# A post-layernorm layer on one core: setup loads as rows, clip logarithms in pieces, and waits by operand

## The reference

```
r = sigmoid(x Wr^T);  k = x Wk^T;  v = x Wv^T
dec = sigmoid(decay);  scale[t] = exp(t * log(clip(dec, 1e-7)))
cum = cumsum(k * v / clip(scale, 1e-10));  state = cum * scale
y = rmsnorm(r * state) * ln_w;  x1 = layernorm(x + y Wo^T)
h = gelu(x1 bw1^T + b1);  out = layernorm(x1 + h bw2^T + b2)
```

## Time and profile before

| | |
|---|---|
| median of 3 runs | 822.54 us (822.36 to 822.7) |
| the profiled execution | 822.86 us |
| its span | 821.0 us |
| busy in the span: PE, DVE, ACT, POOL | 798.2, 772.6, 678.9, 295.6 us |
| granted clock of PE, mean | 0.998 |

### The profile page before, as it was taken

How to read it: one execution, slowest core, us unless ns; L and a number is a source line. 1 busy time by engine, 2 the same in 40 slices (tenths; PEclk the granted TensorE clock), 3 DMA queues, 4 the chain that set the end, 5 groups by cost and what they waited for, 6 DMA issues and landing times.

```text
span 821.0 us, 16564 instructions
## 1 busy us (share of the span) xinstructions
PE 798.2 (97%) x5173; PEld 505.3 (62%) x5173; DVE 772.6 (94%) x1467; ACT 678.9 (83%) x971; POOL 295.6 (36%) x570
## 2 busy tenths in 40 slices
PE   6989999999999999999999999999999999999986
PEld 4555666656666656666656666665666665666653
DVE  7998999999999999999999999999999999999886
ACT  7887888888888888888888888888888888887775
POOL 3343323344323344233344333344332334332344
PEclk9999999999999999999999999999999999999999
DMA  8413554444553434554434554444455344444313
GB/s 249 91 46 78 129 113 94 102 103 102 128 128 83 110 88 102 128 128 92 113 80 109 118 128 103 102 90 108 109 128 112 93 98 106 102 102 103 78 33 97
DMA packets 169847, 86.27 MB, mean 105 GB/s; under 512 B 130145, under 2 KB 165473, under 8 KB 169825
## 3 DMA queue, kind: packets, MB, share of 16 engines
q1 hardware_dynamic: 148304, 52.97, 29.8%
q0 software_dynamic: 4608, 16.78, 10.8%
q10 hardware_dynamic: 16912, 16.26, 5.8%
HBM read 20.45 MB, written 16.78 MB: 45 GB/s over the span
## 4 chain that ended last, share of the span: by engine, by line
PE 89%; DVE 4%; POOL 2%; issue 2%; ACT 2%; DMA 1%; POOLq 0%; DVEq 0%; ACTq 0%; SPq 0%
PE ps_r L362 28%; PE ps_o L483 26%; PE ps_f L433 19%; PE ps_r L433 6%; PE ps_o L388 6%; PE ps_o L393 3%; DVE hid_lo L981 1%; DMA x_in<-in_L_attn_x_dram 1%; DVE u L932 1%; ACT hid L662 1%; DVE u_st L940 0%; PE ps_s L370 0%; POOL root L1284 0%; POOL y_sqs L1272 0%; ACT hid_hi L697 0%
## 5 line engine op out<-in xcount | busy, mean ns | idle before, releaser
L483 PE MATMUL ps_o<-w2T,hid_hi 128*128 128x256 f16 x992 | 218.9, 273 | 3.4 <-DVE hid_lo L981 3.0
L483 PE MATMUL ps_o<-w2T,hid_lo 128*128 128x256 f16 x992 | 218.8, 273 | 0.0
L362 PE MATMUL ps_r<-x_t,proj_hi 128*128 128x512 f16 x768 | 197.1, 379 | 1.7 <-DVE proj_lo L1057 1.2
L433 PE MATMUL ps_f<-x_t,w1T 128*128 128x512 f16 x768 | 181.7, 379 | 1.6 <-DVE x_t L965 1.3
L662 ACT ACTIVATE hid<-ps_f,b1c,f_scale 128x512 f32<-128x512 f32 x192 | 145.3, 774 | 41.6 <-PE ps_f L433 36.6
L981 DVE SCALAR_TENSOR_TENSOR hid_lo<-hid,hid_scale,hid_hi 128x1024 f16<-128x1024 f32 (+1 forms) x136 | 160.3, 1222 | 0.9 <-POOL hid_hi L1305 0.6
L1272 POOL TENSOR_TENSOR y_sqs<-y_sq 128x512 f32<-128x512 f32 x32 | 46.7, 1459 | 308.4 <-ACT y_sq L637 308.4
L362 PEld LDWEIGHTS ps_r<-x_t,proj_hi 128*128 128x128 f16 x768 | 74.5, 98 | 92.1 <-issue 3.4
L697 ACT ACTIVATE hid_hi<-hid,hid_scale 128x2048 f16<-128x2048 f32 (+2 forms) x72 | 128.0, 1778 | 3.2
L433 PEld LDWEIGHTS ps_f<-x_t,w1T 128*128 128x128 f16 x768 | 74.9, 98 | 79.6 <-issue 1.6
L362 PE MATMUL ps_r<-x_t,proj_lo 128*128 128x512 f16 x384 | 114.2, 379 | 0.0
(11 more groups left out here) (182 smaller groups left out, 1333.0 us busy)
## 6 DMA issues: line engine op xcount, KB each, us to landing
x_in<-in_L_attn_x_dram SPq DMA_DIRECT2D x32, 512.0 KB, 4.4
res<-b_row POOLq DMA_DIRECT2D x32, 512.0 KB, 4.6
out_dram<-res ACTq DMA_DIRECT2D x31, 512.0 KB, 3.1
w_in<-in_L_ffn_w_dram SPq DMA_DIRECT2D x2, 1024.0 KB, 10.2
x_t<-x_st SPq DMA_TRANSPOSE x59, 4.3
b_row<-in_L_ffn_b_dram SPq DMA_DIRECT2D x1, 512.0 KB, 13.2
proj_in<-in_L_attn_Wk_dram SPq DMA_DIRECT2D x1, 256.0 KB, 5.2
proj_in<-in_L_attn_Wv_dram SPq DMA_DIRECT2D x1, 256.0 KB, 5.4
```

What stands on the lines that cost most here:

```text
L362: last = nc.tensor.matmul(ps_r[:, m, :], w[:, m, dc, ec * P:(ec + 1) * P], xx[:, :, dc, :], start=(n == 0), stop=(n == 3 * DC - 1))
L433: last = nc.tensor.matmul(f1_bank[hc % NF], w1T[:, hc, dc, :], xx[:, :, dc, :], start=(dc == 0 and n == 0), stop=(dc == DC - 1 and n == 1))
L483: last = nc.tensor.matmul(o_tok[:, tt, :], hh[:, hc, tt * P:(tt + 1) * P], w2T[:, :, hc, :], start=(hc == 0 and n == 0), stop=(hc == HC - ...
```

## The change

decay, ln_w and b1 are loaded by ACT as 2 + 2 + 8 rows of 128 elements into one tile `rows`; PE turns it with one transpose to 128 x 12 (its first instruction, which waits for all three), and DVE copies that from PSUM to `rows_c`, of which decay, ln_w and b1 are now columns. SP issues the load of x first, and its semaphore instructions after the load of x of chunk 2; b1 is no longer in its queue. The squares of chunk 0 move from ACT to DVE. The transposes of chunk 0 go 6 and 2 around the sum of the bound, before 4 and 4, and into banks 1 and 2 of ps_r. clip_g's logarithms are made in four pairs of 512 columns (`clip_logs(n)`), three in the setup and one in the prologue before k_sb of chunk 1; clip_table(0) stands behind proj_split_hi(0). R of chunk 0 waits for proj_hi first, for x lo and for proj_lo only before the products that read them.

```diff
             load(0, 0, 0)
...
             load(2, 0, 2)
-            sp.dma_start(b1c[:, :], b1.rearrange("(c p) -> p c", p=P),
-                         allow_slow_non_contiguous=True).then_inc(s_b1_in, 16)
+            for n in range(CPB):
+                sp.sem_inc(s_stored[n], 16)
+            sp.sem_inc(s_zout, TT)
+            sp.sem_inc(s_xt, 16)
+            sp.sem_inc(s_x1t, 16)
+            sp.sem_inc(s_zadd, 1)
...
                         if first and not ec:
-                            pe.wait_ge(s_setup_ev, m + 1)
+                            pe.wait_ge(s_proj_hi, m + 1)
+                            if m:
+                                pe.wait_ge(s_xl, c + 1)
                         n = 0
                         for w, xx in ((proj_hi, x_split[slot][0]), (proj_hi, x_split[slot][1]),
                                       (proj_lo, x_split[slot][0])):
+                            if first and not ec and not m and n == DC:
+                                pe.wait_ge(s_xl, c + 1)
+                            if first and not ec and n == 2 * DC:
+                                pe.wait_ge(s_setup_ev, m + 1)
...
             def prologue():
+                n = 2 * DC + HC
                 pe.wait_ge(s_ident, 1)
+                pe.wait_ge(s_rows_in, 48)
+                nc.tensor.transpose(ps_rows, rows[:, :], ident[0:n, 0:n]).then_inc(s_rows_t, 1)
                 pe.wait_ge(s_x_in[0], 16)
-                transposes(x_bank[0][:, 0:DC, :], x_in[0], 0, (0, 1))
+                transposes(x_bank[0][:, 0:DC, :], x_in[0], 0, (0, 1, 2))
                 sum_xbound(0)
-                transposes(x_bank[0][:, 0:DC, :], x_in[0], 0, (2, 3)).then_inc(s_tx, 1)
+                transposes(x_bank[0][:, 0:DC, :], x_in[0], 0, (3,)).then_inc(s_tx, 1)
...
-            act.dma_start(dec_c[:, 0, :], decay.rearrange("(c p) -> p c", p=P),
-                          allow_slow_non_contiguous=True).then_inc(s_decay_in, 16)
-            act.dma_start(lnw_c[:, :], ln_w.rearrange("(c p) -> p c", p=P),
-                          allow_slow_non_contiguous=True).then_inc(s_lnw_in, 16)
-            act.wait_ge(s_decay_in, 16)
-            nc.scalar.activation(dec_c[:, 1, :], dec_c[:, 0, :], ACT.Sigmoid).then_inc(s_setup_a, 1)
+            for row, w in ((0, decay), (DC, ln_w), (2 * DC, b1)):
+                n = HC if row == 2 * DC else DC
+                act.dma_start(rows[row:row + n, :], w.rearrange("(c p) -> c p", p=P)).then_inc(s_rows_in, 16)
+            act.wait_ge(s_rows, 1)
+            nc.scalar.activation(dec_c[:, 0, :], rows_c[:, 0:DC], ACT.Sigmoid).then_inc(s_setup_a, 1)
...
             nc.scalar.activation(warm[:, :], ones_col[:, :], ACT.Exp)
-            xsq(0, 0, 0, first=True)
...
             def clip_table(n):
 
-                act.wait_ge(s_clip, DC)
+                act.wait_ge(s_clip, DC * n + DC)
...
             def prologue():
-                clip_table(0)
                 xh(0, 0)
                 proj_split_hi(0)
+                clip_table(0)
                 proj_split_hi(1)
                 clip_table(1)
                 proj_split_hi(2)
...
+            def clip_logs(n):
+
+                dve.wait_ge(s_const, 1)
+                dve.wait_ge(s_setup_a, 2)
+                part = slice(n * CH, (n + 1) * CH)
+                for dc in range(DC):
+                    nc.vector.tensor_scalar(clip_g[:, dc, part], steps[:, part], dec_c[:, 1, dc:dc + 1], -LOG_CLIP,
+                                            ALU.mult, ALU.min).then_inc(s_clip, 1)
+
+            dve.wait_ge(s_rows_t, 1)
+            nc.vector.tensor_copy(rows_c[:, :], ps_rows).then_inc(s_rows, 1)
             dve.wait_ge(s_setup_a, 1)
-            nc.vector.tensor_scalar_max(dec_c[:, 1, :], dec_c[:, 1, :], CLIP_DEC).then_inc(s_setup_v, 1)
...
+            nc.vector.tensor_scalar_max(dec_c[:, 0, :], dec_c[:, 0, :], CLIP_DEC).then_inc(s_setup_v, 1)
+            dve.wait_ge(s_x_in[0], 16)
+            nc.vector.scalar_tensor_tensor(out=x_sq[:, :, :], in0=x_in[0][:, :, :], scalar=1.0, in1=x_in[0][:, :, :],
+                                           op0=ALU.mult, op1=ALU.mult,
+                                           accum_out=bounds[:, DC:DC + 1]).then_inc(s_xsq, 1)
+            proj_maximum(0)
             take_xbound(0, 0)
-            proj_maximum(0)
+            clip_logs(0)
             proj_scale(0)
             proj_maximum(1)
             xl(0, 0)
             proj_scale(1)
             proj_split_lo(0)
             proj_maximum(2)
+            clip_logs(1)
             proj_split_lo(1)
             proj_scale(2)
...
+            clip_logs(2)
             proj_split_lo(2)
...
                 take_bounds(0, 2)
+                clip_logs(3)
                 dve.wait_ge(s_exp, 2 * DC)
                 kvs(1, 1, 0)
```

More of the change, by code:

```diff
@@ L96, in postln_layer_kernel @@
         steps = sb("steps", [P, T])
-        lnw_c = sb("lnw_c", [P, DC])
-        dec_c = sb("dec_c", [P, 3, DC])
+        rows = sb("rows", [2 * DC + HC, P])
+        rows_c = sb("rows_c", [P, 2 * DC + HC])
+        lnw_c = rows_c[:, DC:2 * DC]
+        b1c = rows_c[:, 2 * DC:2 * DC + HC]
+        dec_c = sb("dec_c", [P, 2, DC])
         log_clip = sb("log_clip", [P, 1])
@@ L170, in postln_layer_kernel @@
         o_last = ps_r[:, 0:2, :].rearrange("p a (b d) -> p (a b) d", d=D)
-        x_bank, x_split = [ps_r, ps_o, ps_f], [(x_hi, x_lo), (x1_hi, x1_lo), (x_hi, x_lo)]
+        x_bank, x_split = [ps_r[:, 1:3, :], ps_o, ps_f], [(x_hi, x_lo), (x1_hi, x1_lo), (x_hi, x_lo)]
         ps_sums = ps_s[:, 0:TT * TT]
@@ L177, in postln_layer_kernel @@
         ps_wmax = ps_s[:, TT * TT + DC + 1:TT * TT + DC + 7]
+        ps_rows = ps_s[:, P // 2:P // 2 + 2 * DC + HC]
         ps_womax = ps_f[:, 0, 0:2]
@@ L185, in postln_layer_kernel @@
         s_wo_in, s_w1_in, s_w2_in = (sem(n) for n in ("wo_in_s", "w1_in_s", "w2_in_s"))
-        s_decay_in, s_lnw_in, s_b1_in, s_b2_in = (sem(n) for n in ("decay_in_s", "lnw_in_s", "b1_in_s", "b2_in_s"))
+        s_rows_in, s_rows_t, s_rows, s_b2_in = (sem(n) for n in ("rows_in_s", "rows_t_s", "rows_s", "b2_in_s"))
         s_zeroed, s_ident, s_const = sem("zeroed_s"), sem("ident_s"), sem("const_s")
@@ L264, in load @@
                 sp.dma_start(x_in[j][:, :, :], x_v[c]).then_inc(s_x_in[j], 16)
-            for n in range(CPB):
-                sp.sem_inc(s_stored[n], 16)
-            sp.sem_inc(s_zout, TT)
-            sp.sem_inc(s_xt, 16)
-            sp.sem_inc(s_x1t, 16)
-            sp.sem_inc(s_zadd, 1)
             load(0, 0, 0)
@@ L344, in R @@
                 pe.wait_ge(s_xh, c + 1)
-                pe.wait_ge(s_xl, c + 1)
+                if not first:
+                    pe.wait_ge(s_xl, c + 1)
                 for ec in ecs:
@@ L664, in gelu, with xsq @@
                                          scale=f1_scale[:, hc:hc + 1]).then_inc(s_gelu, 1)
-            def xsq(c, b, j, first=False, looped=False):
+            def xsq(c, b, j, looped=False):
                 act.wait_ge(s_x_in[j], 16 * b + 16)
@@ L670, in xsq @@
                     act.wait_ge(s_bounds, c - 2)
-                elif not first:
+                else:
                     act.wait_ge(s_xbounds, c)
@@ L1069, in _ @@
                                     ALU.add).then_inc(s_fold, 1)
-            dve.wait_ge(s_decay_in, 16)
-            dve.wait_ge(s_setup_a, 1)
-            nc.vector.tensor_scalar_max(dec_c[:, 1, :], dec_c[:, 1, :], CLIP_DEC).then_inc(s_setup_v, 1)
-            dve.wait_ge(s_const, 1)
-            dve.wait_ge(s_setup_a, 2)
-            for dc in range(DC):
-                nc.vector.tensor_scalar(clip_g[:, dc, :], steps[:, :], dec_c[:, 2, dc:dc + 1], -LOG_CLIP, ALU.mult,
-                                        ALU.min).then_inc(s_clip, 1)
+            def clip_logs(n):
[7 more added lines that the diff above has]
+            nc.vector.tensor_copy(rows_c[:, :], ps_rows).then_inc(s_rows, 1)
+            dve.wait_ge(s_setup_a, 1)
+            nc.vector.tensor_scalar_max(dec_c[:, 0, :], dec_c[:, 0, :], CLIP_DEC).then_inc(s_setup_v, 1)
[4 more added lines that the diff above has]
+            proj_maximum(0)
             take_xbound(0, 0)
-            proj_maximum(0)
+            clip_logs(0)
             proj_scale(0)
@@ L1093, in wo_maxima @@
                 dve.wait_ge(s_wo_in, 16)
-                dve.wait_ge(s_lnw_in, 16)
+                dve.wait_ge(s_rows, 1)
                 nc.vector.tensor_reduce(w_max[:, 3:4], wo_in[:, :, :], AX.XY, ALU.max,
@@ L1357, in _ @@
             for dc in range(DC):
-                nc.gpsimd.tensor_scalar(decay_f[:, dc, :], steps[:, 0:CH], 0.0, dec_c[:, 1, dc:dc + 1],
+                nc.gpsimd.tensor_scalar(decay_f[:, dc, :], steps[:, 0:CH], 0.0, dec_c[:, 0, dc:dc + 1],
                                         ALU.mult, ALU.add)
```

6 lines of the change are left out of this document (3 added, 3 removed).

## The result

The changed kernel takes 823.51 us (median of 20 runs, 823.38 to 824.38), the kernel before 822.46 (20 runs in turn with them, 822.31 to 822.70). The ratio is 1.0015, 95% interval 1.0008 to 1.0022: 1.05 us or 0.13% slower, inside the 0.2% that the prediction called no change, and 0.2 us from its 823.3. The profiled execution took 823.39 us with a span of 821.6.

The account below looks back on a forecast made before the run. DVE's setup work up to k_sb of chunk 1 was taken to set the end: 5.71 + 17.25 + 1.28 + 0.38 + 3.6 + 0.3 = 28.52 against 27.62, 0.9 later, so 823.3 us; range 820.8 to 825.3.

Parts of the forecast that it names:

- the long row: PE's long row of second FFN products after the setup, starting at 63.93 before the change, forecast near 64.8.
- What bounds: Setup: DVE runs nearly unbroken from k_sb of chunk 1 to PE's long row, so a k_sb shift moves the end.
- Start of the squares, 5.71: Setup: rows land at 4.3, then transpose, copy, sigmoid and maximum; DVE is free for the squares at 5.71.
- Squares 1.28 and POOL 0.38: Squares of chunk 0 on DVE: 1.28 us, plus 0.38 for POOL writing decay_f beside them.
- The pieces, 3.6: Clip logarithms on DVE: eight operations on 512 columns, some 0.45 each, 3.6 us of new load, the largest term.
- Waits left, 0.3: DVE's waits before k_sb of chunk 1: of 2.7 us, 0.3 is left, 0.2 at the first scale, 0.1 at proj_lo(2).
- The other 17.25: DVE's 19.95 us from x_scl to k_sb of chunk 1, without 2.7 of waits: 17.25 of work with small gaps.
- Waits by operand, 0.4 for PE: PE's first product group: only its last two products need proj_lo now, so PE gains 0.4 us.
- Rival A: Setup on DVE: pieces fill gaps and the start moves with x, 1.7 us faster, 820.8; chance 0.14.
- Rival B: Setup loads: rows land with x at 6.4, delaying DVE and PE by 2.1 us, 825.5; chance 0.22.
- Rival C: Load of x: lands only 0.5 us earlier, at 5.7, ending where the forecast does; chance included in the forecast's.
- PE at half speed: PE's first product group: sign of error if its six products run at half speed, up to 1.3 us.

Follow-up runs that it names:

- e1: Changed kernel with decay loaded into columns ahead of x, chunk 3's clip pair on POOL, rows transposed behind six x transposes, squares back on ScalarE: 822.99 us.
- a3: The changed kernel, but POOL makes the scale of chunk 0 ahead of the two decay_f instructions: 823.11 us.
- b1: The kernel before, with the clip logarithms in four pairs of pieces and ScalarE's exponentials in the changed kernel's order: 824.53 us.
- b2: The kernel before, with x loaded first, TensorE's waits by operand, x transposed into the other banks and ScalarE's x_t ahead of its first exponentials: 823.47 us.
- a2: The changed kernel, but decay is loaded straight into its columns; ln_w and b1 still come as rows, copied only ahead of Wo's maximum: 824.69 us.
- a1: The changed kernel, but VectorE makes the clip logarithms again as two instructions over 2048 columns, where the first pair stood: 824.05 us.

## Why the prediction was right or wrong

The total was right: 28.52 forecast for k_sb of chunk 1, 28.66 measured; 64.8 for the long row, 64.94 measured; 823.3, 823.51 measured. The steps were not equally good: the start was right to 0.03, but I had the squares 0.52 too high, the rest of DVE's work 0.44 too high, the pieces 0.70 too low and the waits 0.37 too low. That these cancel to 0.14 is luck; that DVE's added work sets the shift is not, as the runs show.

- *What bounds:* right. Thirteen kernels have 36.3 us from k_sb of chunk 1 to the long row, and the fourteenth (e1) that and a gap that its trace shows.
- *Start of the squares, 5.71:* measured 5.74, by errors that met: the rows landed at 4.80 (forecast 4.3), but from start to start transpose to copy took 0.29 (4.93 to 5.22, forecast 0.42), sigmoid to maximum 0.23 (forecast 0.32), and maximum to squares 0.08, where I had added its duration in the earlier trace rows, 0.29.
- *Squares 1.28 and POOL 0.38:* from the squares' start to the next operation 1.14 went by (5.74 to 6.88), not 1.66. The pair shared with POOL cost the other engine: decay_f took 2.25, against 1.38 in the earlier trace rows, and the first clip piece, beside its second half, 939 ns against 470. The Trainium skill ("SBUF — State Buffer", on the two separate sides) says that whoever starts first holds the ports for the whole instruction. The squares started first (5.74, decay_f 5.95), and of decay_f's two halves the first took 1.57 and the second 0.70; so the trace agrees, and my added 0.38 was put on the wrong engine. The sum by that rule, 0.3 to 1.0 higher, was not what came, since I had assumed that POOL starts first.
- *The pieces, 3.6:* measured from start to start 1.26, 0.78, 0.93 and 1.33 (27.33 to 28.66), 4.3 together. This is the term that was too small: the two pairs that ran beside POOL, the first (decay_f) and the last (y_sqs), were 0.36 and 0.43 over my 0.9, the other two near it. The single piece was right (470 ns; forecast 0.45).
- *Waits left, 0.3:* x_t 0.43, y_q 0.24. The wait for x_t was the chain over POOL: I had its scale ready at 8.8, and it was ready at 8.93 by way of decay_f, with the last table covered at 8.46 to 8.66. I named decay_f as something that runs beside DVE and missed that the scale stands behind it on POOL's own queue (a3: 0.28).
- *The other 17.25:* these remainders leave 16.81 (28.66 - 5.74 - 1.14 - 4.30 - 0.67). It was too high by 0.44. Most of it, by estimate, is the overlap of 0.08 between neighbours that comes back with each wait that goes.
- *Waits by operand, 0.4 for PE:* worth 0.65 in k_sb, between its two halves of chunk 0, a place that I did not name; ahead of that nothing, as the pieces had filled the wait already (b1, b2).
- *Rival A (DVE has room)* fell: pieces of 0.47 are over its 0.32, and DVE started on x at 5.74, not by 5.0.
- *Rival B (rows land with x)* did not come, at 4.80 against its deciding point of 5.0, but a2 shows its mechanism at work: 4.6 us for decay in 256 pieces beside x, and 6.39 for the last rows.
- *Rival C:* the load of x took 3.5 us and landed at 4.2 (forecast 4.5), not at 5.7; this did not matter, as forecast.
- *PE at half speed:* not in the changed kernel, whose first product group took 1.03; a1 shows it, at some 0.5 us.
- *At the end:* the last normalisation is 1.39 later (DVE's at 818.38, before 816.99), since the aggregation at 814.02 waits 0.53 where the one of before did not; the profiled spans differ by 0.6 only (821.6 against 821.0), so the final stores gave the rest back, for a reason that stays open.
